# A fused Perceiver layer: two phases in one block, VectorE's first step reordered, x1 loads and root chains moved

## The reference

```python
x = x + xattn(layernorm(x), ctx, ctx, wq, wk, wv, wo)      # one head, 256 context rows + the 64 own
x = x + attn(layernorm(x), W_Q, b_Q, W_K, b_K, W_V, b_V, W_O, b_O)  # 16 heads of 128, rope, causal
x = x + ffn(layernorm(x), gate_up fp4 codes and scales, down fp4 codes and scales)
# ffn: h = silu(gate) * up over 1408; y = h @ w_down.T; y / sqrt(mean(y * y) + 1e-6)
```

## Time and profile before

| what | value |
|---|---|
| three executions | 1358.47, 1357.62, 1357.37 us; median 1357.62 |
| the profiled execution, its time | 1361.96 us |
| its span, first to last instruction | 1359.9 us |
| TensorE busy | 1332.6 us, 98% |
| VectorE busy | 1006.8 us, 74% |
| ScalarE busy | 508.5 us, 37% |
| GpSimd busy | 383.5 us, 28% |
| mean granted TensorE clock | 0.996 |

### The profile page before, as it was taken

One profiled execution on the slowest core, in us unless ns is written; L12 is line 12 of the kernel. 1 busy time (PEld: TensorE's weight loads), 2 busy tenths in 40 slices (PEclk: granted clock), 3 DMA queues, 4 the chain that ended last, 5 costly groups with the idle time before them and its releaser, 6 DMA issues. The chain is left out here.

```text
span 1359.9 us, 23419 instructions
## 1 busy us (share of the span) xinstructions
PE 1332.6 (98%) x9216; PEld 773.3 (57%) x9216; DVE 1006.8 (74%) x2295; ACT 508.5 (37%) x1260; POOL 383.5 (28%) x304
## 2 busy tenths in 40 slices
PE   8999999999999999999999999999899999999998
PEld 6666666645666666666666666654344434434443
DVE  6444444278988888887888877849998799688684
ACT  4222222243333434333343333320001576666661
POOL 0000000021222222222222222213042396748481
PEclk9999999999999999999999999999999999999999
DMA  9555554541000221102201024336841000000001
GB/s 342 209 205 202 202 186 186 217 178 47 33 32 16 63 63 32 32 17 63 63 32 33 16 63 155 94 84 188 194 162 62 1 1 1 1 1 32 1 32 62
DMA packets 41765, 122.56 MB, mean 90 GB/s; under 512 B 4280, under 2 KB 6968, under 8 KB 34232
## 3 DMA queue, kind: packets, MB, share of 16 engines
q1 hardware_dynamic: 40488, 118.19, 25.8%
q10 hardware_dynamic: 1168, 2.88, 1.1%
HBM read 95.89 MB, written 25.17 MB: 89 GB/s over the span
## 5 line engine op out<-in xcount | busy, mean ns | idle before, releaser
L191 PE MATMUL psum<-xt_hi,hqk_hi 128*128 128x512 f16 x512 | 194.4, 380 | 1.7 <-PEq L215 1.7
L193 PE MATMUL psum<-xt_hi,hqk_lo 128*128 128x512 f16 x512 | 194.0, 379 | 0.0
L192 PE MATMUL psum<-xt_lo,hqk_hi 128*128 128x512 f16 x512 | 194.0, 379 | 0.0
L904 POOL TENSOR_TENSOR hd_rotated<-hd_products 64x512 f32<-64x512 f32 x32 | 40.4, 1262 | 422.3 <-DVE hd_products L1168 422.3
L1565 POOL TENSOR_TENSOR ff_part<-ff_part 128x512 f32<-128x512 f32 x88 | 129.9, 1478 | 83.1 <-DVE ff_part L1697 82.7
L1697 DVE SCALAR_TENSOR_TENSOR ff_part<-psum,gu_scale,ff_part 128x512 f32<-128x512 f32 x176 | 122.8, 742 | 36.7 <-PE psum L1591 31.1
L191 PE MATMUL psum<-hd_wv_hi,xt_hi 128*128 128x256 f16 x512 | 139.5, 273 | 0.0
L193 PE MATMUL psum<-hd_wv_hi,xt_lo 128*128 128x256 f16 x512 | 139.5, 273 | 0.0
L192 PE MATMUL psum<-hd_wv_lo,xt_hi 128*128 128x256 f16 x512 | 139.5, 273 | 0.0
L1590 PE MATMUL psum<-xt_hi,gu 128*128 128x512 f16 x352 | 134.2, 381 | 5.4 <-DVE ff_part L1697 4.8
L1591 PE MATMUL psum<-xt_lo,gu 128*128 128x512 f16 x352 | 134.1, 381 | 0.0
(11 more groups left out here) (196 smaller groups left out, 3072.2 us busy)
## 6 DMA issues: line engine op xcount, KB each, us to landing
xa_kv_t<-in_ctx_t_dram SPq DMA_DIRECT2D x16, 1024.0 KB, 5.5
xa_kv<-in_ctx_dram SPq DMA_DIRECT2D x16, 1024.0 KB, 4.9
w_rows<-in_head_weights_dram SPq DMA_DIRECT2D x10, 1024.0 KB, 8.1
z_scratch<-hd_z_hi SPq DMA_DIRECT2D x32, 256.0 KB, 2.7
z_scratch<-hd_z_lo SPq DMA_DIRECT2D x32, 256.0 KB, 3.4
hqk_lo<-z_scratch SPq DMA_DIRECT2D x8, 1024.0 KB, 8.4
w_rows<-z_scratch SPq DMA_DIRECT2D x8, 1024.0 KB, 8.4
xn<-in_x_dram SPq DMA_DIRECT2D x8, 512.0 KB, 3.8
```

Of the source, the lines that this page charges most:

```text
L191: pe.matmul(out, lh, rh, start=(first and i == 0), stop=False)
L192: pe.matmul(out, lh, rl, start=False, stop=False)
L193: last = pe.matmul(out, ll, rh, start=False, stop=(final and i == k - 1))
```

## The change

Both phases' functions take the block as an argument and no longer open their own; one block is opened around both calls. In the heads, VectorE scales the biases ahead of its wait for the x1 stores, and the last two `low_wv` of the second column group come behind the sum-up of the first step. In the merge, `load_x1(2)` is issued in the next turn of SP's loop. In the feed-forward, root_start, root_end and the four finish come six units later.

```diff
--- before.py
+++ after.py
@@ -204,7 +204,7 @@
 NH = TOK // HALF_TILE
 
 
-def xattn_phase(nc, psum, ident, x_rows, ctx_kv, ctx_t, wq, wk, wv, wo, identity, x1_rows, w_hi, w_lo, w_rows, xn, stat,
+def xattn_phase(nc, block, psum, ident, x_rows, ctx_kv, ctx_t, wq, wk, wv, wo, identity, x1_rows, w_hi, w_lo, w_rows, xn, stat,
                 head_weights, hqk_hi, hqk_lo, rows_loaded, x1_stored, x1_t_hi, x1_t_lo, tables, tables_in, tables_loaded, late_rows_loaded):
 
 
@@ -274,8 +274,6 @@
 
         def block_of(i):
             return slice(i * P, (i + 1) * P)
-
-        block = ctx.enter_context(nc.Block())
 
         @block.sync
         def _(sp):
@@ -807,7 +805,7 @@
     return z_scratch[hi_or_lo, t, half, :, :, :].rearrange("d (a h) t -> d a h t", h=2)
 
 
-def heads_phase(nc, psum, ident, x1_rows, xn, stat, hqk_hi, hqk_lo, w_rows, w_o, wo_hi, wo_lo, z_scratch, first_z, small_loaded_z_stored,
+def heads_phase(nc, block, psum, ident, x1_rows, xn, stat, hqk_hi, hqk_lo, w_rows, w_o, wo_hi, wo_lo, z_scratch, first_z, small_loaded_z_stored,
                 early, early_sems, b_o, shifts, gu_scales, gu_codes, first_rows_loaded, x1_stored,
                 xt_hi, xt_lo, cos, sin, mask, bias, bias_v, late_rows_loaded):
 
@@ -1139,6 +1135,11 @@
                     dve.wait_ge(xt_hi_done, nth * KD + (k + 1))
                     banks.moves(dve.tensor_tensor(xt_lo[:, k, :], psum_of(("x", k)), xt_hi[:, k, :], ALU.subtract), ("x", k))
 
+            dve.wait_ge(small_loaded_z_stored, 16 * HEADS_SMALL)
+            dve.tensor_scalar(bias[:, :, :, :].rearrange("p a b q -> p (a b q)"), bias[:, :, :, :].rearrange("p a b q -> p (a b q)"),
+                              XS * WS, None, ALU.mult).then_inc(bias_scaled, 1)
+            dve.tensor_scalar(bias_v[:, :], bias_v[:, :], AS, None, ALU.mult).then_inc(bias_scaled, 1)
+            dve.wait_ge(bias_scaled, 2)
             wait_x1_stored(dve)
 
             def low_wv(c, k):
@@ -1147,11 +1148,6 @@
                 dve.scalar_tensor_tensor(wv_lo[:, k, cols], wv_rows[k][:, cols], WS, wv_hi[:, k, cols],
                                          ALU.mult, ALU.subtract).then_inc(w_lo_done, 1)
 
-            dve.wait_ge(small_loaded_z_stored, 16 * HEADS_SMALL)
-            dve.tensor_scalar(bias[:, :, :, :].rearrange("p a b q -> p (a b q)"), bias[:, :, :, :].rearrange("p a b q -> p (a b q)"),
-                              XS * WS, None, ALU.mult).then_inc(bias_scaled, 1)
-            dve.tensor_scalar(bias_v[:, :], bias_v[:, :], AS, None, ALU.mult).then_inc(bias_scaled, 1)
-            dve.wait_ge(bias_scaled, 2)
             for k in range(KD):
                 low_wv(0, k)
 
@@ -1235,9 +1231,6 @@
                     low_wv(1, 1)
                 if s.proj:
                     multiply(s, 1, 0)
-                    if not s.att:
-                        low_wv(1, 2)
-                        low_wv(1, 3)
                     multiply(s, 1, 1)
                     if s.att:
                         side_work(s)
@@ -1251,6 +1244,8 @@
                 if s.proj:
                     low_values(s.a + 1, 0)
                 if not s.att:
+                    low_wv(1, 2)
+                    low_wv(1, 3)
                     for k in range(KD):
                         low_wv(2, k)
                 elif s.t == 0 and s.pair in (0, 1, 2):
@@ -1350,14 +1345,13 @@
                 sp.wait_ge(z_used[1], t)
                 load_z(t, 1)
                 if t == 2:
+                    load_x1(2)
                     load_x1(3)
                     load_down()
                 if t == NT - 2:
                     sp.wait_ge(z_stored, 16 * (HEADS_SMALL + 2 * NT * PAIRS))
                 sp.wait_ge(z_used[0], t)
                 load_z(t + 1, 0)
-                if t == 1:
-                    load_x1(2)
             sp.wait_ge(z_used[1], NT - 1)
             load_z(NT - 1, 1)
 
@@ -1755,12 +1749,12 @@
                     if u in (8, 10, 12, 14):
                         scale_block(t + 1, u // 2 - 4)
                 if t >= 2:
-                    if u == 5:
+                    if u == 11:
                         root_start(t - 2, 0, TT)
-                    if u == 7:
+                    if u == 13:
                         root_end(0, TT)
-                    if u in (9, 11, 13, 15):
-                        finish(t - 2, (u - 9) // 2)
+                    if u in (15, 17, 19, 21):
+                        finish(t - 2, (u - 15) // 2)
 
             second_halves(0)
             for t in range(NT):
@@ -1805,12 +1799,13 @@
         cos, sin, mask = (sb(n, [P, S], F32) for n in ("cos", "sin", "mask"))
         bias, bias_v = sb("bias", [P, 2, 2, PAIRS], F32), sb("bias_v", [P, HEADS], F32)
         tables = (cos[:, :], sin[:, :], mask[:, :], bias[:, 0, :, :], bias[:, 1, :, :], bias_v[:, :])
-        xattn_phase(nc, psum, ident, x.rearrange("b s d -> (b s) d"), ctx_2048, ctx_t, wq, wk, wv, wo,
-                    identity, x1, wo_hi, wo_lo, w_rows, xn, stat, head_weights, hqk_hi, hqk_lo,
-                    rows_loaded, x1_stored, xt_hi, xt_lo, tables, (rope_cos, rope_sin, causal, b_q, b_k, b_v), z_stored, late_rows_loaded)
-        heads_phase(nc, psum, ident, x1, xn, stat, hqk_hi, hqk_lo, w_rows, w_o, wo_hi, wo_lo, z, first_z, z_stored,
-                    early, early_sems, b_o, shifts, gu_scales, gu_codes, rows_loaded, x1_stored,
-                    xt_hi, xt_lo, cos, sin, mask, bias, bias_v, late_rows_loaded)
+        with nc.Block() as block:
+            xattn_phase(nc, block, psum, ident, x.rearrange("b s d -> (b s) d"), ctx_2048, ctx_t, wq, wk, wv, wo,
+                        identity, x1, wo_hi, wo_lo, w_rows, xn, stat, head_weights, hqk_hi, hqk_lo,
+                        rows_loaded, x1_stored, xt_hi, xt_lo, tables, (rope_cos, rope_sin, causal, b_q, b_k, b_v), z_stored, late_rows_loaded)
+            heads_phase(nc, block, psum, ident, x1, xn, stat, hqk_hi, hqk_lo, w_rows, w_o, wo_hi, wo_lo, z, first_z, z_stored,
+                        early, early_sems, b_o, shifts, gu_scales, gu_codes, rows_loaded, x1_stored,
+                        xt_hi, xt_lo, cos, sin, mask, bias, bias_v, late_rows_loaded)
         gu, gu_scale = sb("gu", [P, KD, GU], F16), sb("gu_scale", [P, 2 * FB * KD], F32)
         down_hi, down_lo = sb("down_hi", [P, FB, D], F16), sb("down_lo", [P, FB, D], F16)
         merge_phase(nc, psum, z, x1, wo_hi, wo_lo, gu_codes, down_codes, down_scales,
```

## The result

| | before | after |
|---|---|---|
| median of the executions | 1357.49 us (4: 1355.93 to 1358.47) | 1351.00 us (4: 1350.34 to 1351.75) |
| the profiled execution, its time | 1361.96 us | 1350.34 us |
| its span | 1359.9 us | 1348.5 us |
| mean granted TensorE clock | 0.996 | 0.999 |

A forecast was written before the change was run, and what follows sets the result against it. TensorE, busy for 98% of the span, bounds the kernel, so only its waits can give. First step 1.5 + x1 loads 0 + root chains 2.0 = 3.5 us, median 1357.62 to 1354.1; range 1349.5 to 1356.2.

The forecast's parts named there:

- rival 1: Merge: the x1(2) load did hold z back; 1351.4 us, or 1348.5 if wait and low clock go; chance 0.18.
- the root chains' term: Feed-forward, tile 2: moving the chains six units later cuts TensorE's wait from 2.5 to 0.5 us, gain 2.0.
- Rival 3: Feed-forward: the root chains' wait only moves, or the first step gives under 0.9; 1355.2 to 1356.5 us; chance 0.14.
- rival 4: Feed-forward, units 11 to 17: the root chains take twice as long beside GpSimd; slower, 1360.1 us; chance 0.04.
- The x1 loads: 0.: Merge: issuing load_x1(2) later gains 0, since each DMA engine takes its queue in order and x1 stands behind z.
- The 4.1 us before L799 unchanged, and the clock's fall too: Merge, sign in the profile: TensorE's 4.1 us wait for z stays, and the granted clock still falls.
- One block: 0.: Phase boundary: removing TensorE's 1.70 us wait gains 0, since VectorE's chain sets L1043 and the wait at L1027 grows.
- (a): First step of the heads: bias scalings ahead of the x1 wait start VectorE's chain earlier; gain 0.6 us.
- (b): First step of the heads: low_wv(1,2) and (1,3) behind the sum-up take 0.7 us instead of 2.8; gain 2.1.
- (c): First step of the heads: VectorE's sum-up now meets GpSimd's and stands until it ends; loss 1.2 us, other end 0.
- The wait foretold at L1043: First step of the heads: TensorE's wait there grows from 0.5 to about 1.2 us.
- Rival 2: First step of the heads: VectorE's sum-up is not held by GpSimd's; 1.2 us more gain, 1352.9 us; chance 0.10.

## Why the prediction was right, and where it was wrong

*Direction and place of the two main parts* were right: the first step gained on VectorE's chain, though mostly not by the terms of the forecast, and the root chains gained by a wait in tile 2 that went away and came back only as 0.36 us. The total was 3 us too small. That 1351.0 still lies in the stated range is partly luck: the range was that wide for the rivals' sake, and the value fell beside the price of rival 1, whose mechanism did not hold. In the profiles the first step gives 1.8 us and the root chains 2.7 to 4.4; that is 4.5 to 6.2, and the medians say 6.5 and 6.9 (8.6 against the other timing of the kernel before). What is left between them, 0.3 to 2.4 us without this last, isn't placed. The edits timed one by one add up to 4.3 us (ratios 0.999, 0.9996 and 0.9982), less than all together, but each of these is near what the measurement gives for the same kernel.

*The step that failed is the root chains' term*, "Gain 2.5 - 0.5 = 2.0". Its wait part was right: the waits on L1697 went from 4.8 to 2.7 us, one of 0.36 is left at unit 16. It left two things out. The clock fell to the 1.2 GHz level behind the 2.2 us wait in four of the five executions that had this wait (252.0 to 252.3 us against 250.6 without the fall): 1.6 us. And each stop costs 0.22 us beyond its idle time. With the 2.1 us of idle time these make 3.9 of the 4.3 or 4.4 us; the rest isn't placed. The forecast had taken this very effect into account behind the z wait and never asked for the windows behind the other long wait. Rival 3, that the wait only moves, is refuted; so is rival 4.

*The x1 loads: 0.* Right as the edit's worth within 2 us, by the loads moved alone and by the kernel with x1(2) put back; right too in its reason that the codes on the other queue hold up half of the engines. What the forecast expected of the profile, "The 4.1 us before L799 unchanged, and the clock's fall too", was wrong, and by its own words ("Wrong if the L799 wait shrinks by over 1 us") the pair of profiles spoke for rival 1. Only the second execution of the kernel before, with 2.0 us and no fall, showed that a wait of this size comes and goes from execution to execution at this one place.

*One block: 0.* Right in its reason, that VectorE's chain sets L1043: with the block alone the chain started where it had. But the 1.7 us were not given back at L1027 as foretold; that wait grew by 0.2 only, since the chain itself became 1.3 us shorter. In three of four executions with the barrier three of the four low_wv were held by GpSimd, in the fourth two, and none in any of the ten without it. So 1.4 us went with the block in the profiles. That the barrier causes it isn't shown: with the barrier in place the kernel with only the x1 loads moved, an edit far behind this step, gained 1.0 us here in the same way. What decides isn't shown either: low_wv(1,0) started 0.23 us ahead of GpSimd's sum-up in all of them.

*The first step's terms.* (a) Bias: 0.6 forecast, 0.5 measured. (b) low_wv moved, 2.1: nothing, by the kernel that put it back. The 2.1 was the price of the collision, and this had already gone in the kernel with the block alone. (c) VectorE's sum-up held, -1.2: -1.2, but spread over two instructions, and already -1.9 with the block alone. That the sum of 1.5 came near 1.85 is luck, two errors that cancel: the block too low by 1.4, (b) too high by 2.1, with (c) charged to the move of low_wv. The wait foretold at L1043, "about 1.2 us", was 1.18. Rival 2 is refuted: the sum-up was held.

The Trainium skill, page "SBUF — State Buffer", section "SBUF: two separate sides", has whichever of VectorE's instruction with two SBUF inputs and GpSimd's starts first keep the port and the other wait. The kernel before fits that in who was held: the low_wv that took longer, 1.50 us, started at 300.76, behind GpSimd's 300.66, and the one ahead of it, from 300.43, took its 0.41. So far the changed kernel fits too, as low_wv starts at 298.61 and GpSimd at 298.84 takes 1.66. But the second low_wv, at 298.94, was not held, though it stands as far behind GpSimd as the held one of before; nor was the one at 302.40 in the kernel with the block alone, 0.04 us behind GpSimd's 302.36, which took 1.93. Who goes next when both have been waiting, or start within 0.1 us of each other, isn't shown by these runs.

## What to carry to other kernels

A long stop of TensorE has to be priced with the windows of the granted clock right behind it; here the fall was worth 1.6 us where the wait was 2.2. Before a saving is read out of one pair of profiles, the same kernel should be profiled twice: the z wait was 4.1 us in one and 2.0 in the other. When the price of a moved instruction is a collision, ask whether the collision stays once the neighbouring edit is made, and read uneven DMA shares (5 of 10 with a queue waiting) as a load that can be spread.

## What the runs showed of the hardware that was not expected

Who is held when VectorE and GpSimd both read SBUF repeated to 0.01 us between two executions of the same program (1.83 and 1.82, 1.49 and 1.50). It was otherwise in all ten executions without the barrier, and in one with it, whose only edit lay some 650 us later. Behind cross attention TensorE's clock fell behind stops of 4.09 and 2.28 us and behind four of five of 2.2 us; it didn't behind 1.99 us, nor behind any of 1.7 or less. In the first 20 us, where each execution has a stop of 2.0 to 2.6 us ending near 14 us, it fell in ten of fourteen, behind one of 2.09 and not behind two of 2.55 and 2.56; L425 came at 276.8 to 278.3 us in those ten, at 275.8 to 276.7 in the others. That is a spread of up to 2.5 us that no edit here touches.
